# GpSimd operations of 1024 and 768 columns issued as operations on 256 columns, in a two-layer gated MLP kernel

## The reference, cut to what matters

```python
xn = layernorm(x)                                   # 4 x 512 tokens, 1024 features
s  = silu(xn @ Wg_a.T)                              # 2752 hidden features ("A")
s  = where(|s| is among the 1376 smallest of its row, 0, s)
s  = (s * (xn @ Wu_a.T)) @ Wd_a.T
g  = silu((silu(xn @ Wg_b.T) * (xn @ Wu_b.T)) @ Wd_b.T)   # 2752 hidden features ("B")
out = x + s * g
```

## Time and profile before

| | us |
|---|---|
| median of 3 runs | 2782.82 (2781.74 to 2786.43) |
| the profiled execution, its own time | 2784.59 |
| its span | 2782.8 |
| TensorE busy in the span | 2753.9 |
| VectorE busy | 2307.4 |
| GpSimd busy | 388.3 |

### The profile page before, as it was taken

One profiled execution on the slowest core, in us unless ns is written; L12 is line 12 of the kernel. 1 busy time (PEld: TensorE's weight loads), 2 busy tenths in 40 slices (PEclk: granted clock), 3 DMA queues, 4 the chain that ended last, 5 costly groups with the idle time before them and its releaser, 6 DMA issues. The chain is left out here.

```text
span 2782.8 us, 31374 instructions
## 1 busy us (share of the span) xinstructions
PE 2753.9 (99%) x12204; PEld 2281.1 (82%) x12204; DVE 2307.4 (83%) x3002; ACT 1352.7 (49%) x1386; POOL 388.3 (14%) x161
## 2 busy tenths in 40 slices
PE   9999999999999999999999999999999999999999
PEld 7778888878788888888878888888887888888887
DVE  7676999999967698998986678999897767999971
ACT  4234998332444477631144557671115446776110
POOL 5565443044400000000020000000011000000000
PEclk9999999999999999999999999999999999999999
DMA  6898888579766555556656655555666664555564
GB/s 235 308 328 286 293 288 280 211 251 357 255 193 196 181 188 192 189 203 219 249 190 195 192 180 190 195 196 194 240 223 195 193 196 173 195 196 193 189 233 170
DMA packets 135097, 614.28 MB, mean 221 GB/s; under 512 B 12752, under 2 KB 12752, under 8 KB 89168
## 3 DMA queue, kind: packets, MB, share of 16 engines
q1 hardware_dynamic: 134992, 612.94, 63.2%
HBM read 492.31 MB, written 120.59 MB: 220 GB/s over the span
## 5 line engine op out<-in xcount | busy, mean ns | idle before, releaser
L632 PE MATMUL ps<-w_split,hid_ring 128*128 128x512 f32 x4096 | 935.2, 390 | 6.8 <-ACT hid_buf L1136 4.6
L632 PEld LDWEIGHTS ps<-w_split,hid_ring 128*128 128x128 f32 x4096 | 769.4, 188 | 171.5 <-issue 7.9
L1380 DVE TENSOR_SCALAR_CACHE_REDUCE ranks<-key_buf,cand 128x2752 int16<-128x2752 f32 x248 | 762.9, 3076 | 5.8
L961 ACT ACTIVATE signs_row<-key_buf,cand 128x2752 bf16<-128x2752 f32 x248 | 642.6, 2591 | 191.6 <-DVE cand L1389 182.0
L877 PE MATMUL ps<-xnT,w_split 128*128 128x512 f32 x1376 | 535.3, 389 | 0.0
L876 PE MATMUL ps<-xnT,w_split 128*128 128x512 f32 x1376 | 535.3, 389 | 0.0
L875 PE MATMUL ps<-xnT,w_split 128*128 128x512 f32 x1376 | 535.3, 389 | 0.0
L1206 POOL TENSOR_TENSOR w_split<-w_raw,w_split 128x1024 fp32r<-128x1024 f32 (+2 forms) x118 | 290.2, 2467 | 377.3 <-ACT w_split L928 137.0
L875 PEld LDWEIGHTS ps<-xnT,w_split 128*128 128x128 f32 x1376 | 258.3, 188 | 53.7
L876 PEld LDWEIGHTS ps<-xnT,w_split 128*128 128x128 f32 x1376 | 258.3, 188 | 53.6
L877 PEld LDWEIGHTS ps<-xnT,w_split 128*128 128x128 f32 x1376 | 258.3, 188 | 53.3
(11 more groups left out here) (146 smaller groups left out, 2907.0 us busy)
## 6 DMA issues: line engine op xcount, KB each, us to landing
w_split<-split SPq DMA_DIRECT2D x272, 1024.0 KB, 4.8
split<-w_split SPq DMA_DIRECT2D x72, 1024.0 KB, 6.8
w_raw<-w_a SPq DMA_DIRECT2D x100, 512.0 KB, 4.2
w_raw<-t_dram SPq DMA_DIRECT2D x78, 512.0 KB, 3.3
w_raw<-w_b SPq DMA_DIRECT2D x42, 512.0 KB, 4.9
w_extra_raw<-t_dram SPq DMA_DIRECT2D x42, 512.0 KB, 3.6
t_dram<-t_buf SPq DMA_DIRECT2D x20, 1024.0 KB, 8.6
w_extra_raw<-w_a SPq DMA_DIRECT2D x30, 512.0 KB, 3.6
```

Of the source, the lines that this page charges most:

```text
L632: ins = pe.matmul(ps[:, 2 * t + half, :], h, w[:, half * TB:(half + 1) * TB], start=(first and n == 0), stop=last and stop)
L961: act.activation(signs_row[:, :], keys[:, t, :], ACT.Sign, bias=cand_f[:, t:t + 1], scale=-1.0, accum_out=counts[:, t:t + 1]).then_inc(act ...
L1380: dve.tensor_scalar(ranks[:, :], keys[:, t, :], cand_f[:, t:t + 1], 0.0, ALU.is_lt, ALU.add, accum_out=counts[:, t:t + 1]).then_inc(sel_st ...
```

## The change

Each GpSimd operation of `low`, `low_stage`, `s_sum` and the additions of the output is replaced by operations on 256 columns each, one behind the other, of which the last alone signals the semaphore. An operation on 1024 columns becomes four, one on 768 three; the two on 512 columns in `low` become two each. Nothing moves on any other engine, and no wait is added or removed.

```diff
+PIECE = 256
+
+def pieces(w):
+    return [slice(c, c + PIECE) for c in range(0, w, PIECE)]
...
                 pool.wait_ge(hi_ready, splits_before(b, m) + 1)
-                pool.tensor_tensor(w_lo[q][:, 0:w], w_raw[q][:, 0:w], w_hi[q][:, 0:w].bitcast(F32),
-                                   ALU.subtract).then_inc(lo_ready, 1)
+                for cols in pieces(w):
+                    ins = pool.tensor_tensor(w_lo[q][:, cols], w_raw[q][:, cols], w_hi[q][:, cols].bitcast(F32), ALU.subtract)
+                ins.then_inc(lo_ready, 1)
...
                 pool.wait_ge(stage_hi, s + 1)
-                pool.tensor_tensor(stage[:, 1, :], w_stage_raw[s % STAGES][:, :], stage[:, 0, :].bitcast(F32),
-                                   ALU.subtract).then_inc(stage_lo, 1)
+                for cols in pieces(H):
+                    ins = pool.tensor_tensor(stage[:, 1, cols], w_stage_raw[s % STAGES][:, cols], stage[:, 0, cols].bitcast(F32),
+                                             ALU.subtract)
+                ins.then_inc(stage_lo, 1)
...
+            def s_chunks(out, in0, in1, op):
+
+                for k in range(4):
+                    ins = pool.tensor_tensor(out[:, k, :], in0[:, k, :], in1[:, k, :], op)
+                ins.then_inc(s_raw, 1)
...
-                    pool.tensor_tensor(s_row(1), s_feat(0, tok2), s_feat(1, tok2), ALU.add).then_inc(s_raw, 1)
+                    s_chunks(s_row(1), s_feat(0, tok2), s_feat(1, tok2), ALU.add)
...
                     pool.wait_ge(ad_free, b * NT + (NT + t + 1))
-                    pool.tensor_tensor(x_res[:, t, :], x_res[:, t, :], silu_g[:, t, :], ALU.add).then_inc(out_ready, 1)
+                    for cols in pieces(H):
+                        ins = pool.tensor_tensor(x_res[:, t, cols], x_res[:, t, cols], silu_g[:, t, cols], ALU.add)
+                    ins.then_inc(out_ready, 1)
```

More of the change, by code:

```diff
@@ L1226, in s_sum @@
                 if n == 0:
-                    pool.tensor_tensor(s_row(1), s_feat(0, tok2), s_feat(1, tok2), ALU.add).then_inc(s_raw, 1)
+                    s_chunks(s_row(1), s_feat(0, tok2), s_feat(1, tok2), ALU.add)
                 elif n == 1:
                     pool.wait_ge(s_raw, (b - 1) * 4 + 1)
-                    pool.tensor_tensor(s_row(0), s_row(1), s_feat(0, tok1), ALU.subtract).then_inc(s_raw, 1)
+                    s_chunks(s_row(0), s_row(1), s_feat(0, tok1), ALU.subtract)
                 elif n == 2:
-                    pool.tensor_tensor(s_row(2), s_feat(0, tok1), s_feat(0, tok2), ALU.subtract).then_inc(s_raw, 1)
+                    s_chunks(s_row(2), s_feat(0, tok1), s_feat(0, tok2), ALU.subtract)
                 else:
                     pool.wait_ge(s_raw, (b - 1) * 4 + 3)
-                    pool.tensor_tensor(s_row(3), s_feat(1, tok1), s_row(0), ALU.subtract).then_inc(s_raw, 1)
+                    s_chunks(s_row(3), s_feat(1, tok1), s_row(0), ALU.subtract)
             for m in range(TILES):
```

## The result

The changed kernel takes 2820.09 us, the median of four runs (2815.49 to 2821.5), where the kernel before takes 2782.84 (2781.74 to 2786.43): ratio 1.0132, 95% interval 1.012 to 1.0145. It is slower by 37 us. I had forecast 2796 and a range up to 2807: the sign was right, the size was not, and the range did not hold it. The profiled execution took 2815.49 us (span 2813.7), 30.9 more than that of before. It is the fastest of its four runs, and that of before was 1.8 us above its median, so 6 us of the 37 are in no trace; of them I can only say that the other three runs were granted a TensorE clock of 0.990 to 0.992 over the span, the profiled one 0.993.

A forecast was written before the change was run, and what follows sets the result against it. TensorE was taken as the bound, with GpSimd mattering only where others wait for it. Block 0's 0 and the seams' 16 us, less a us per seam for gaps, made 13: 2782.8 + 13 = 2796, range 2775 to 2807.

The forecast's parts named there:

- The price of a piece: On GpSimd, 256 columns take 0.70 us, bounds 0.59 and 0.80; four pieces cost 0.46 us more than one whole operation.
- The turns: Where VectorE has two-input work queued, each piece lets one operation in, costing GpSimd 0.43 us (512 columns) or 0.96 (1024).
- the wait in front of P5: Blocks 1 to 3: TensorE waits some 6 us for `s_lo` before P5, with a lower clock behind.
- the freed VectorE decides: Rival: VectorE, blocked for less time, makes block 0 and the seams faster, 13 us in all, to 2770; chance 0.13.
- (a): Block 0, stage A: 3.6 us gained at 192 us, low-part waits longer by 1.3; together -1, bounds -4 and +3.
- Seams: Three block seams: a late third addition delays P5, 16 us in all, bounds 0 and 24; 3.1 + 2 from 1 to 2.
- gaps in which GpSimd would get two pieces in a row: At each seam, one gap where VectorE waits for a high part takes a us off the loss.
- (b): Block 0, from BD to AD: TensorE waits 4.6 us behind VectorE's late transposes; 2 us regained, bounds 0 and 8.
- (c): Block 0, end of AD: TensorE follows GpSimd's slower sums and low parts; 4 us lost, bounds 2 and 7, net 3.
- a sign against me: Block 0: the forecast is wrong if TensorE's wait in front of AD goes away altogether.
- GpSimd keeps its port from piece to piece: Rival: VectorE waits as before or longer, each split operation costs 0.46 us; 14 us slower, 2797; chance 0.08.
- the straight line of the prediction: GpSimd's time by columns: 2.2 ns a column plus 0.18 us per operation, drawn from operations on 512 and 1024 columns.

The follow-up runs named there:

- experiment 1: The changed kernel with the output's additions whole again, all other GpSimd work in pieces; 2797.36 us, 1.0056 to the kernel before.
- experiment 2: The kernel before with only the output's additions in pieces of 256 columns; 2803.63 us, 1.0076.
- experiment 5: The changed kernel with VectorE waiting at each seam, behind `xn_low`, for the third addition; 2799.76 us, 1.0064 to the kernel before.
- Experiment 4: The changed kernel, all pieces kept, with each staged tile's store one ring tile later in SyncE's queue; 2799.57 us, 1.0064 to the kernel before.
- its control: The kernel before, nothing in pieces, with each staged tile's store one ring tile later in SyncE's queue; 2777.59 us, 0.9982.
- experiment 12: The kernel before with only stage A's `low` operations of block 0 in pieces; 2792.05 us, 1.0031.
- Experiment 7: The changed kernel with the staged tile's store one ring tile later in SyncE's queue and the output's additions whole; 2781.06 us, 0.9991 to the kernel before.

## Why the prediction was wrong

**What held.** The price of a piece (0.70). The turns: one VectorE operation behind each piece, 14.05 us worked out for the seam's twelve pieces and 14.23 measured; in the middle of the blocks nothing changed. `s_hi(1)` at the end of the third addition; the wait in front of P5 at each of three seams. The sign of each place but one. Experiments 1, 2 and 5 show that it was this chain and that its cause is the turns. The lock for a whole instruction of the Trainium skill (SBUF — State Buffer, Who interferes with whom), which spoke for the rival that the freed VectorE decides, holds as far as it goes: `xn_low`'s pair fell from 4.92 to 2.06 us. But P5 waited for the chain behind the third addition, not for a blocked VectorE.

**The step that failed: (a), stage A of block 0, "Together -1, bounds -4 and +3".** It measured +10.8. In the trace I was off by 17.9 us (2815.49 against 2784.59 + 13), and 11.8 of them are this step (without it the median would have come to some 2808, still just above the range). I counted VectorE's two blocked operations and TensorE's direct waits for low parts, which I let grow by 1.3 us and which grew from 3.4 to 11.6, and left out the queue: `spill_stage` waits for `low_stage` ahead of loads of raw tiles, so a longer `low` can come back one tile later as a later raw tile, a later high part and a later `low`. The rows to see it were there. SyncE's queue had waited 49.5 us for GpSimd in that stretch, and I had asked for that view at the seams only. Experiment 4 and its control show the queue's part: 10.8 us with it, 2.4 without; experiment 12 shows that `low` is the main source. How a `low` that is 1 us longer becomes 3.5 us of waiting at 82 us and 4.0 at 226, while the waits between are short, I followed at one place only.

**Seams: sized 16, measured 21.4.** Same mechanism, two terms too small. For the seam from 1 to 2 I had 3.1 + 2. The load of a = 7 took 4.9 us until ScalarE could use it and not 4.1, and a = 8 came 0.55 us late as well, so that P5 started 27.2 us after VectorE's first product, not 25.5: 1.7 us. And its 24 matmuls lost 2.8 us to the lower clock (8.47 less 5.69), where I had charged 2: behind 7.69 us of idleness, longer than the 4.55 that I went by. 5.1 + 1.7 + 0.8 = 7.6, measured 7.5. I had also taken 3 us off the sum for gaps in which GpSimd would get two pieces in a row; the twelve pieces took 14.20 to 14.23 us at each seam, which shows none worth a term.

**(b) and (c).** From BD to AD 2.9 us came back where I counted 2 (the "10 us" that I named there are 3.6 + 5, so 8.6; no term used them); the wait in front of AD all but vanished (4.55 to 0.44), which I had named as a sign against me. It was not one: two short waits of 0.96 and 0.98 us came up inside BD instead. At the end of AD the loss was 1.7 instead of 3, the wait of 4.8 us for a low part at 723.84 included.

**The 6 us outside the traces** I had not allowed for.

## What to carry to other kernels

Where GpSimd and VectorE share a stretch, the end of each GpSimd instruction is a turn that VectorE may take: cutting one into four traded one long wait of VectorE for up to four delays of GpSimd, so count who waits for GpSimd's *last* piece before cutting. Then look at the in-order DMA queue of the same stretch: a store that waits for that engine ahead of loads can turn a small delay into a late tile, and moving the store back one place (edit 4) gave back 20.5 of the 37 us. And when an edit cures a loss, run it on the kernel before too: by the medians a quarter of that gain was the order's own, by the start of B nearly half.

## What the runs showed that I had not expected

The turns are not always taken. At the end of AD, VectorE's timeline of the changed kernel:

```profile
731.50 10.70 DVE L1363 TENSOR_TENSOR xnT<-prods,xnT 128x512 fp32r<-128x512 f32 x3 [8.30 <-ACT xnT L953]
```

and GpSimd's beside it:

```profile
729.26 2.83 POOL L1236 TENSOR_TENSOR prods<-prods 128x256 f32<-128x256 f32 x4
732.05 2.82 POOL L1214 TENSOR_TENSOR w_split<-w_raw,w_split 128x256 fp32r<-128x256 f32 x4
734.83 2.83 POOL L1236 TENSOR_TENSOR prods<-prods 128x256 f32<-128x256 f32 x4
737.61 2.83 POOL L1214 TENSOR_TENSOR w_split<-w_raw,w_split 128x256 fp32r<-128x256 f32 x4
```

The first of VectorE's three took 9.50 us, until GpSimd's run of pieces ended at 740.44: some thirteen pieces went by undisturbed, 0.70 apart, while it stood ready. Experiment 7 shows the same, 10.71 us for the three; experiments 1, 4 and 5 at the same place don't, and neither does the changed kernel itself ten microseconds earlier, where each of VectorE's took 1.2 us. It is the behaviour of the rival that I had given 0.08 ("GpSimd keeps its port from piece to piece"), in one place. What decides between the two I did not find, and no run was made for it.

The price of a small GpSimd instruction came out near the straight line of the prediction: four pieces took 2.81 us against 2.37 for the whole one, 0.44 us more, where the line gave 0.46. The estimate that the prediction worked out from the Trainium skill (GPSIMD Engine Reference, Performance pitfalls for Q7 kernels), 0.51, is a little too much.
